# A binarised 3x3 convolution on one core: the input copied one pair further ahead, the statistics split round the sums, the filter solve woven into the start

## What is computed

```python
An  = sign(clip(gn(x) + v[n], 0, 1) - 0.5)          # n = 0, 1, 2
B   = sign(W - mean(W) + us[m] * std(W))            # m = 0..4, us = -1, -0.5, 0, 0.5, 1
alpha = solve(Bf.T @ Bf, Bf.T @ W)                  # a 5 x 5 system
W_eff = sum over m of alpha[m] * B[m]               # 3 x 3 x 32 x 32
out = x + sum over n of beta[n] * (conv3x3(An, W_eff) + sum(alpha) * bias[n])
```

## Time and profile before

| | |
|---|---|
| median of 3 runs | 207.09 us (206.98 to 207.84) |
| the profiled execution's own time | 206.35 us |
| its span, first to last instruction | 204.6 us |
| mean granted TensorE clock | 0.995 |
| busy, share of the span: PE, DVE, ACT, POOL | 82%, 84%, 68%, 31% |

### The profile page before, as it was taken

How to read it: one execution, slowest core, us unless ns; L and a number is a source line. 1 busy time by engine, 2 the same in 40 slices (tenths; PEclk the granted TensorE clock), 3 DMA queues, 4 the chain that set the end, 5 groups by cost and what they waited for, 6 DMA issues and landing times.

```text
span 204.6 us, 4766 instructions
## 1 busy us (share of the span) xinstructions
PE 167.0 (82%) x1800; PEld 128.9 (63%) x1800; DVE 171.6 (84%) x422; ACT 139.9 (68%) x183; POOL 62.7 (31%) x76
## 2 busy tenths in 40 slices
PE   1596166489898989898989898989899999789871
PEld 0484065266767676767676767777777776658560
DVE  5449999998999999999999999999999999875241
ACT  2626557287888878787878787878787878673110
POOL 6174243543333333232323232414141414240000
PEclk9999999999999999999999999999999999999998
DMA  4799333061688979797889787978797464657625
GB/s 113 228 268 272 94 81 85 0 163 51 193 233 240 265 215 262 212 256 221 239 240 262 216 254 226 255 224 253 227 251 229 131 187 137 181 149 211 194 67 157
DMA packets 21030, 39.61 MB, mean 194 GB/s; under 512 B 9744, under 2 KB 9744, under 8 KB 21008
## 3 DMA queue, kind: packets, MB, share of 16 engines
q1 hardware_dynamic: 20272, 39.27, 67.9%
q10 hardware_dynamic: 736, 0.04, 0.2%
HBM read 13.15 MB, written 12.85 MB: 127 GB/s over the span
## 4 chain that ended last, share of the span: by engine, by line
PE 49%; ACT 19%; DVE 16%; issue 7%; DMA 6%; SPq 2%; ACTq 0%; DVEq 0%
PE conv_ps L723 24%; PE y_ps L743 13%; ACT signs L348 13%; PE x_ps L685 9%; ACT y_ch L361 6%; DMA x_nat<-in_x 4%; DMA s_odd<-s_even 3%; DVE raw_stats L555 2%; DVE y_nat L546 2%; DVE twice_dev L582 1%; DVE s_even L612 1%; DVE s_even L617 1%; PE x_ps L693 1%; DVE neg_thr L591 1%; PE conv_ps L782 1%
## 5 line engine op out<-in xcount | busy, mean ns | idle before, releaser
L723 PE MATMUL conv_ps<-s_even,w_mm 128*64 128x448 f16 (+1 forms) x576 | 102.9, 332 | 3.0 <-DVE w_mm L518 1.6
L726 PE MATMUL conv_ps<-s_odd,w_mm 128*64 128x448 f16 (+2 forms) x576 | 102.9, 320 | 0.0
L348 ACT ACTIVATE signs<-x_ch,neg_thr 128x784 f16<-128x784 f32 x96 | 85.0, 940 | 2.2 <-DVE neg_thr L591 2.2
L723 PEld LDWEIGHTS conv_ps<-s_even,w_mm 128*64 128x64 f16 x576 | 60.5, 110 | 30.4 <-issue 5.0
L726 PEld LDWEIGHTS conv_ps<-s_odd,w_mm 128*64 128x64 f16 x576 | 60.6, 110 | 0.0
L546 DVE SCALAR_TENSOR_TENSOR y_nat<-y_ps,y_const,x_nat 112x1024 f32<-112x1024 f32 (+1 forms) x32 | 36.6, 1145 | 10.2 <-PE y_ps L743 10.2
L306 POOL TENSOR_SCALAR lo_part<-signs,ratio_lo 128x1568 f16<-128x1568 f16 x16 | 25.5, 1595 | 62.3 <-ACT signs L348 62.2
L685 PE MATMUL x_ps<-ident,x_nat 112*128 112x112 f32 x224 | 31.8, 290 | 13.4 <-ACT x_ch L343 10.1
L743 PE MATMUL y_ps<-ident,y_ch 128*112 128x128 f32 x224 | 31.2, 279 | 11.3 <-ACT y_ch L361 9.9
L310 POOL TENSOR_SCALAR lo_part<-signs,ratio_lo 128x1568 f16<-128x1568 f16 x16 | 26.6, 1664 | 44.9 <-DVE half_hi L605 44.9
L343 ACT ACTIVATE x_ch<-x_ps 128x896 f32<-128x896 f32 (+1 forms) x32 | 26.1, 815 | 19.5 <-PE x_ps L685 19.5
(11 more groups left out here) (106 smaller groups left out, 92.5 us busy)
## 6 DMA issues: line engine op xcount, KB each, us to landing
x_nat<-in_x SPq DMA_DIRECT2D x16, 448.0 KB, 5.1
out<-y_nat SPq DMA_DIRECT2D x16, 448.0 KB, 3.8
s_odd<-s_even SPq DMA_DIRECT2D x32, 203.0 KB, 2.8
s_odd<-s_even SPq DMA_DIRECT2D x32, 188.5 KB, 3.0
x_nat<-in_x SPq DMA_DIRECT2D x16, 336.0 KB, 4.7
out<-y_nat SPq DMA_DIRECT2D x16, 322.0 KB, 2.6
s_odd<-s_even SPq DMA_DIRECT2D x32, 14.5 KB, 2.7
x_nat<-in_x SPq DMA_DIRECT2D x16, 14.0 KB, 5.3
```

What stands on the lines that cost most here:

```text
L348: act.activation(signs[q % 2][:, n, :, a, :], x_ch[q % CH_SLOTS][:, :, a, :], ACT.Sign, bias=neg_thr[q % 2][:, n, a:a + 1]).then_inc(signe ...
L723: last = nc.tensor.matmul(low[:, 0:n * ROWS], wt, s_even[b][:, part, r0:r0 + 2 * n, t:t + H], start=first, stop=end)
L726: last = nc.tensor.matmul(high[:, 0:m * ROWS], wt, s_odd[b][:, part, r0:r0 + 2 * m, t:t + H], start=first, stop=end and not at_edge)
```

## The change

- **Order of a round on ACT.** `copy_in` is for pair p+5, and `scale_out(p+1, 0)` stands between its two halves, ahead of the first sign pair, where it stood behind it. PE brings in pair p+5. The slots of `x_nat` and `x_ch` go from 6 and 3 to 7 and 4.
- **Order of a round on DVE.** `lane_moments(p+4, 0)` moves in front of `sum_high`, and `sum_low` from behind `add_x(p, 1)` to between `invert_root` and `divide_variance`, ahead of the thresholds.
- **Start-up.** The three parameter vectors are loaded to one partition and spread to 128 by a matmul, copied by DVE (`params_ready`). Pairs 0 to 3 use `y_ps` and `conv_ps[1]` beside `x_ps` for the way in. The elimination is woven between the statistics and thresholds of pair 0, and pair 0's sums, pair 1's thresholds and the filter are written out in one sequence; the steps begin at -1. The filter's five weightings of 192 elements become one product of 960 elements (`w_parts`) and one reduction over it.

The core of the diff:

```diff
-LEAD = 4
-X_SLOTS, CH_SLOTS, S_SLOTS = 6, 3, 3
+X_SLOTS, CH_SLOTS, S_SLOTS = 7, 4, 3
...
-            act.dma_start(params[:, 1, :], v.partition_broadcast(128)).then_inc(params_loaded, 16)
-            act.dma_start(params[:, 0, :], beta.partition_broadcast(128)).then_inc(params_loaded, 16)
-            act.dma_start(params[:, 2, :], bias.partition_broadcast(128)).then_inc(bias_loaded, 16)
+            for i, t in enumerate((beta, v, bias)):
+                act.dma_start(params_row[:, i, :], t.unsqueeze(0)).then_inc(params_loaded, 16)
...
                 if real(p + 3):
                     take_root(p + 3)
-                if real(p + LEAD):
-                    copy_in(p + LEAD, 0)
-                    copy_in(p + LEAD, 1)
+                if real(p + 5):
+                    copy_in(p + 5, 0)
+                if real(p + 1):
+                    scale_out(p + 1, 0)
+                if real(p + 5):
+                    copy_in(p + 5, 1)
                 if real(p + 3):
                     begin_signs(p + 3)
-                if p == -1:
-                    act.wait_ge(y_scale_ready, 1)
-                if real(p + 1):
-                    scale_out(p + 1, 0)
...
+            def weigh_filters():
+                dve.wait_ge(corners_zero, 2)
+                settle()
+                fl = filt[:].rearrange("p a o c m -> p (a o c) m")[:, :, 0:M_FIL]
+                mark(stt(w_stat[:, 6:11], neg_alpha, -1.0, neg_alpha, ALU.mult, ALU.max))
+                return mark(tt(w_parts[:], fl, neg_alpha.unsqueeze(1).broadcast_to([128, TAPS * 2 * C, M_FIL]),
+                               ALU.mult))
+
+            def sum_filters(n):
+                settle(n)
                 mark(nc.vector.reduce_sum(size[:, 0:1], w_stat[:, 6:11], axis=AX.X))
+                return mark(nc.vector.reduce_sum(w_eff[:].rearrange("p a o c -> p (a o c)"), w_parts[:], axis=AX.X))
...
             def step(p):
-                q, r, t = p + 2, p + 3, p + LEAD
+                q, r, t = p + 2, p + 3, p + 4
...
                 if real(r):
                     pair_moments(r)
+                if real(t):
+                    lane_moments(t, 0)
                 if real(q):
                     sum_high(q)
                 if real(r):
-                    make_thresholds(r, add_root(divide_variance(r, invert_root(r))))
+                    n = invert_root(r)
+                if real(q):
+                    sum_low(q)
+                if real(r):
+                    make_thresholds(r, add_root(divide_variance(r, n)))
                 if real(p):
                     add_x(p, 1)
-                if real(q):
-                    sum_low(q)
-                if p == -2:
-                    filter_parts()
                 if real(t):
-                    lane_moments(t, 0)
                     lane_moments(t, 1)
                     spread_lanes(t)
...
+            weigh_first(0)
+            substitute(3)
+            substitute(2)
+            weigh_second(0)
+            sum_half(0)
+            substitute(1)
+            pair_moments(1)
+            sum_high(0)
+            n = invert_root(1)
+            sum_low(0)
+            n = divide_variance(1, n)
+            k = weigh_filters()
+            n = add_root(n)
+            k = sum_filters(k)
+            make_thresholds(1, n)
+            filter_sizes(k)
+            split_filters()
+            lane_moments(2, 0)
+            lane_moments(2, 1)
+            spread_lanes(2)
+            output_const()
+            for p in range(-1, PAIRS):
                 step(p)
...
-                if real(p + LEAD):
-                    bring_in(p + LEAD, 0)
+                if real(p + 5):
+                    bring_in(p + 5, 0)
                 if real(p + 3) and p != -1:
                     gather_lanes(p + 3)
                 if real(p + 1):
                     convolve(p + 1, 0)
...
+            pe.wait_ge(params_loaded, 48)
+            nc.tensor.matmul(params_ps, ones[0:1, :], params_row[:].rearrange("p i n -> p (i n)"),
+                             start=True, stop=True).then_inc(params_spread, 1)
```

More of the change, by code:

```diff
@@ L790, in _ @@
                              start=True, stop=True).then_inc(gram_summed, 1)
[L791 to L792 removed]
+            pe.wait_ge(same_ch_ready, 1)
+            pe.wait_ge(x_copied, 1)
+            gather_lanes(0)
+            bring_in(1, 1, y_ps, 2)
+            pe.wait_ge(moments_ready, 2)
+            bring_in(2, 0, x_ps, 3)
+            bring_in(2, 1, conv_ps[1], 3)
+            pe.wait_ge(x_copied, 5)
+            gather_lanes(1)
+            bring_in(3, 0, y_ps, 5)
+            pe.wait_ge(moments_ready, 4)
+            bring_in(3, 1, x_ps, 6)
+            pe.wait_ge(hi_made, 1)
+            for _ in range(WARM):
+                nc.tensor.matmul(conv_ps[0][:, 1, 0:128], ones[:], ones[:], start=True, stop=True)
+            for p in range(-1, PAIRS):
                 step(p)
```

155 lines of the change are left out of this document (83 added, 72 removed).

## The result

The changed kernel takes **212.7 us** (median of 4 runs, 211.51 to 214.51) against 207.31 us (206.98 to 207.84, 4 runs) for the kernel before: ratio 1.0265, 95% interval 1.0187 to 1.0342. It is slower, as forecast, but by 5.4 us and not by 2.8. The profiled execution took 212.5 us with a span of 210.7.

A forecast was written before the change was run, and what follows sets the result against it. PE, with one 0.63 gap, set the 10.34 round; after the change a DVE loop held by POOL would set 10.64. Start-up 0, rounds +3.6 and end -0.8 gave +2.8 on 207.09, so 209.9 us, range 207.7 to 211.6.

The forecast's parts named there:

- Part 1: ACT's order in the middle rounds: PE's 0.63 wait at the way out goes, round 9.71 if nothing else bound.
- Parts 2 and 3: Middle rounds: the loop through DVE takes 10.21; POOL's first weighting holds `spread_stats`, making it 10.64, +3.6 over twelve rounds.
- Part 5: End of the kernel: last round +0.2, pair 15's scaling -0.45, earlier `sum_low` 0.6 gained; sum -0.8, bounds -1.5 and 0.
- Part 4: Start-up: pair 2's first signs at 42.5 for 42.25, taken as about 0, bounds -1.0 and +1.2.
- the filter's work ahead of pair 1's thresholds: Start-up on DVE: product and reduction of 960 elements taken as 1.13 each with 0.1 between, 2.36 in all.
- the -0.7 for the parameters: Start-up: the parameters' 384 small DMA packets go, gaining 0.7, bounds 0 and -1.5.
- the matmul that spreads the parameters: Start-up: it, DVE's copy and three DMA issues lie beside other work, so they add no time.
- a further wait: Rival for the rounds: gather waits behind PE's longer queue or shifts come late; round 10.85, +5.3, 212.4; chance 0.05.
- No hold: Rival for the middle rounds: POOL does not hold DVE there; round 10.21, total 204.7; chance 0.17.

The follow-up runs named there:

- act_old: dve_warm with `scale_out(p + 1, 0)` behind the first sign pair again, as before the change; 207.5 us, ratio 1.0005.
- dve_warm: The changed kernel with the old order in VectorE's round and 26 warming products in place of 4; 203.6 us, ratio 0.9836.
- thr_first: dve_warm with 15 warming products and pair 1's thresholds made ahead of the filter's product and reduction; 201.6 us, ratio 0.9753.
- after again: The changed kernel unaltered, run and profiled a second time; 212.4 us, ratio 1.0271 to the kernel before.
- warm26 again: The changed kernel with 26 warming products in place of 4, run a second time on the chip of after again; 210.5 us, ratio 1.0170.
- pool_one: The changed kernel with POOL's first weighting of each pair cut from 1568 columns to one; 206.5 us, ratio 0.9971.
- before_warm0: The kernel before the change without its four warming products; 208.5 us, ratio 1.0028.
- warm0: The changed kernel without its four warming products; 211.1 us, ratio 1.0210.
- all_behind: thr_first with 12 more products behind pair 2's gather and the parameters' product moved behind pair 0's way in; 203.1 us, ratio 0.9786.
- low_early: thr_first with `sum_low` ahead of the thresholds, as in the changed kernel; 202.1 us, ratio 0.9771.

## Why the prediction was right and wrong

- **Part 1**: right in its mechanism. The wait at the way out is gone; act_old against dve_warm gives 0.36 to 0.4 a round for it, not the 0.63 that holds if nothing else binds.
- **Parts 2 and 3**: right to 0.04. 10.60 for 10.64 with the hold, 10.19 for 10.21 without. `spread_stats` at 1.42, `sum_high` at 0.96, TensorE's wait at the gather.
- **Part 5**: -0.8 came, in both profiles of the changed kernel. With 26 warming products and the same order it is -0.2 and 0, since the last shifts land later. The 0.6 that part 5 kept for `sum_low` hangs on that landing, so it is in part luck.
- **Part 4 is the step that failed**, in the term "PE (way in 0.77, then half 0 of pair 0, 18 x 0.19 + 0.15 = 3.6". These are prices of the middle rounds, at full clock, set into a place where TensorE had just been without work for 6 us. Measured, from start to start: the way in 1.65, half 0 up to the gather 4.89, with seven pairs 0.375 apart; with the clock held up 0.88 and 3.57. From pair 1's signs to pair 2's 11.9 was forecast, 14.27 came, and 12.20 with the clock held up. The rows to see it by stood in before's timeline too: the same way in (8 blocks) takes 1.73 in its start-up and 0.93 in the middle, and its warming products are followed at once by a way in and 1.6 us later by the convolution, where the change puts a wait of 6 us between. I had priced the gap on TensorE at nothing, since no clock below 1.00 stood in before's windows.
- **A second term of part 4 is too small**: the filter's work ahead of pair 1's thresholds. Its product took 1.88 (1.79 to the next start), where 1.13 was taken and 1.5 was the upper bound; with the reduction and the small instructions between it is 3.1 us, where 2.36 was taken, and thr_first gets 3.0 back. Pair 0's signs came at 17.51, 0.65 earlier than before, so the -0.7 for the parameters was met in this profile. From there to pair 1's signs it was 14.3 in every profile with this start, 3.1 longer than before's 11.20, where 31.3 - 29.36 = 1.9 was forecast. In eight later profiles with this start pair 1's signs stand at 29.8 to 31.4, mean 30.7, against a forecast of 30.6, but that is luck: pair 0's came a further 1.1 us earlier there on average (16.4), and the two errors cancel.
- The words "the matmul that spreads the parameters ... lie beside other work" are wrong too: pair 0's signs follow the row's landing, which moves by 1.8 us between executions.
- At pair 2's signs the miss of the first profile is 3.5 us: 2.1 the clock, 1.1 the way from pair 0's signs to pair 1's, 0.3 not assigned. The rounds give 0.5 of it back. Of the 2.8 us between the forecast's 209.9 and the median of 212.7, keeping the clock up takes away 1.6 on one chip (after again against warm26 again) and 2.5 between the two first results (212.7, 210.2), which come from different chips.
- The rival *a further wait* (212.4) came nearest by its number, but by a mechanism that is not there: the rounds are not 10.85. *No hold* has its check in pool_one, whose round of 10.19 is the 10.21 it rests on.

## What to carry to other kernels

A price read in a steady stretch holds in the start-up only if TensorE comes to it as busy: when a change opens a gap ahead of matmuls, look where the warming work stands and fill the gap with it (that fewer products at the gap's end would do is untried here), and look whether the clock falls again at the next gap. In a loop between two engines, what is placed ahead of the value that the other engine waits for costs what the loop then has over the fullest queue: 1.94 us of VectorE's work cost 0.27 a round here. It can also shift small two-input instructions of VectorE into GpSimd's long ones, which cost 0.43 more. The costs do not add up simply, so try each piece alone. One change may hold a gain and a loss: here the eviction between the copies (-0.4 a round) was hidden under VectorE's new order (+0.7), and with the old order there, the thresholds first and the clock kept up the kernel takes 201.0 us, ratio 0.9739 (0.9683 to 0.9794) to the one before.

## What the runs showed of the hardware that was not expected

- The granted clock of a trace is not to be believed ahead of its first change. In before_warm0 the windows from 34 to 38 us show 1.00, and the products there stand 0.375 apart; the start-up of before, with 1.00 throughout, has ways in of 8 blocks of 1.73 where the middle rounds have 0.93. So its mean clock of 0.995 is too high, and cannot be set against the 0.942 of the changed kernel. The spacing of equal products tells the clock more surely.
- The clock can rise while TensorE has already stopped: 0.68 in 28 to 30 and 1.00 in 30 to 32, where no product ran, and 0.50 again when the work came. Four warming products (1.94 us) followed by 6 us of nothing gained nothing (warm0 without them is not slower); 26 of them brought pair 2's signs 2.0 us nearer to pair 1's.
- A shift within SBUF mostly lands 3.1 us after its issue, but single ones took 6.32 and 5.99 (all_behind), 5.43 (low_early) and 5.03 (warm26 again), and TensorE stood still for up to 1.74 us for one.
